# Spreading the keys by heads on Pool in the second attention, and scaling the first batch's probabilities earlier in Pool's queue

## The chip, the cores and the metric

The kernel runs on one core of one Trainium2 chip. The metric is the device time of one execution in microseconds (us). The engines have short names here: PE is TensorE (matmuls), ACT is ScalarE, DVE is VectorE, Pool is GpSimd, SP issues the DMAs. Every engine runs its own queue of instructions in order; they meet only at semaphores.

## What is computed

Four layers, each a cross attention and a feed-forward part, act on x (32 batches of 64 tokens, 128 wide) with a context of the same size. The parts that matter here, cut from the reference:

```python
def _L0_xattn_ref(image_embeds, latents, ...):       # front: 16 heads of 64
    ...
    w = jnp.einsum('bhqd,bhkd->bhqk', q * scale, k * scale)
    w = jax.nn.softmax(w.astype(jnp.float32), axis=-1).astype(q.dtype)
    ...
def _L1_ffn_ref(x, ...):                             # mixture of experts, 2 of 8
    ...
    for _ in range(NUM_ITER):
        ...
        hidden = _gelu(jnp.einsum('tc,tch->th', ctx_e, w1) + b1)
    ...
def _L2_xattn_ref(query, key, value, Wq, bq, Wk, bk, Wv, bv, Wo, bo):
    q = (query @ Wq.T + bq).reshape(B, T, H, D).transpose(0, 2, 1, 3)
    k = (key @ Wk.T + bk).reshape(B, S, H, D).transpose(0, 2, 1, 3)   # H = 16, D = 8
    ...
    scores = jnp.einsum('bhtd,bhsd->bhts', q, k) / np.sqrt(D)
    scores = scores + causal[None, None]
    attn = jax.nn.softmax(scores, axis=-1)
    out = jnp.einsum('bhts,bhsd->bhtd', attn, v)
```

The layers run as x = x + xattn0, x + ffn0, x + xattn1, x + ffn1 (the experts), x + xattn2, x + ffn2, x + xattn3, x + ffn3.

## The kernel before

**Tiling.** A tile is 128 tokens (two batches); there are 16 tiles. Products go to eight PSUM banks. For each bank there is a semaphore that counts fills (`bank_full`) and one that counts emptyings (`bank_free`). The helper `filled` waits until a job's product lies in its bank; `stored` waits until the engine that empties the bank has finished writing the result. Each engine's order is a list written by hand of (kind, lag): in step n, kind works on tile n - lag.

**Front (about 0 to 355 us).** Layer 0 and the attention of layer 1 are one software pipeline with the lists FRONT_PE, FRONT_ACT, FRONT_DVE and FRONT_POOL (L669 to L679). For a tile's two batches b = 0 and 1, PE forms the scores (L812), DVE takes the negated maxima (L1010), ACT the exponentials and their sums (L910), DVE the reciprocals of the sums (L1016, kinds inv0 and inv1), Pool multiplies the exponentials by them (`probs`, L1100, two instructions of 128x512 for each batch, kinds probs0 and probs1), and PE turns the result (L764, kinds turn0 and turn1). A norm is moments on DVE (L507, L512), its root on Pool (two instructions, L517 adds epsilon and L520 takes the power -1/2), and its application on DVE (L526). In a full step Pool's list before is root2, own, ctx (two roots), root1, again, probs0, root0, probs1, bias0, bias1, so five roots stand between the step's own norm and probs0: own, the two of ctx, root1 and again.

**Mixture of experts (about 345 to 620 us).** Chunks of 512 tokens, four chunks and two iterations, with PE, ACT and DVE in hand-written turns. In iteration 0 PE spreads the one-hot routing of a chunk into seven masks (L1556), ACT copies each into SBUF (L1636), DVE multiplies the hidden values by it (L1749). Before the change ACT then waits for its own copy (`stored`) and raises a second semaphore, f1_kept, on which DVE waits.

**Second attention (layer 2, about 600 to 710 us; n == 2 in `attention`).** The last turns of the experts are merged with its first tiles by hand (PE_END, ACT_END, DVE_END, POOL_END, L1285 to L1295); then the steps of ATT_PE, ATT_ACT, ATT_DVE and ATT_POOL (L1299 to L1302) run, and the lists DRAIN_* end it. In a step PE runs s, lnt, v, ot, t, out, av, qk, lnt0: the scores of a tile (L1980 adds the causal mask, L1988 the products), turning the norm (L639), values (L2003), turning the output (L2010), turning the probabilities (kind t, L2018), the output product (L2024), the weighted values (L2037), the projected keys and queries (kind qk, L2046 and L2048, two lags ahead of their use in s), and another norm. ACT runs lnt, v, ot, t, qk, lnt0, s. DVE runs own, max (L2116), tail (L526), add (L576, waits for L2024), s (L2126, scores less their maximum), rsum, stats, av, apply (L526). ACT's kind s is the exponential (L2103), and PE's t waits for it.

Four heads lie in the 32 rows of a PE quadrant, so the keys are stored four times in `km`, each copy multiplied by the column of `head4` that keeps one head's rows. Before the change ACT does this straight from PSUM, four instructions (L2096), and stores the queries with a fifth (L2098):

```python
for h in range(QUAD):
    nc.scalar.activation(km[:, u, :, h, :], ps(k, P, P)..., ACT.Identity,
                         bias=bk2[:, h:h + 1], scale=head4[:, h:h + 1])
nc.scalar.activation(qT2[:, u, :], ps(k, P), ACT.Identity, ...).then_inc(free[k], 1)
```

`bk2` is the key bias times head4, built once on DVE. The fourth attention (n == 3) builds its keys elsewhere (L1933).

## Time and profile before

| | us |
|---|---|
| median of 3 runs (lowest, highest) | 862.83 (862.62, 863.03) |
| the profiled execution's own time | 861.2 |
| its span in the trace | 859.1 |
| PE busy | 809.4 (94% of the span) |
| DVE busy | 625.2 (73%) |
| ACT busy | 581.3 (68%) |
| Pool busy | 271.1 (32%) |

The clock granted to TensorE is 0.998 of full speed over the span. The chain that ended last is PE 60%, DVE 13%, ACT 12%, Pool 8%, issue 5% of the span. Its largest pieces on ACT are the exponentials and the four key copies of the second attention (L2096, 3%), on Pool the roots (L520, 3%) and the scaling of probabilities (L1100, 2%).

To read a row of a timeline: start in us from the span's start, length, engine, line, instruction, output<-inputs, shapes, how many in a row were merged, and in brackets the engine's idle time before it with what ended it. Successive instructions of one engine overlap a little in the records, so the distance of two starts is what one costs its engine.

### The profile page before, as it was taken

The numbers are of one execution on the slowest core, as the hardware profiler recorded it, in microseconds if no ns is written. First come the engines' busy times: TensorE is split into PE (matmuls) and PEld (weight loads), VectorE is DVE, ScalarE is ACT, GpSimd is POOL, SyncE is SP. The second block draws the span as 40 slices with busy tenths as digits, with TensorE's granted clock in tenths as the row PEclk, the third lists the DMA queues.
The fourth block names the chain that finished last, engine by engine and source line by source line (L and its number), as shares of the span: only waits on it lengthen the run. The fifth ranks groups of instructions, "written<-read, shape, count | busy, mean of one in ns | idle before, by whom it ended". The sixth has DMA issues, their size and how long they took to land.

```text
span 859.1 us, 20341 instructions
## 1 busy us (share of the span) xinstructions
PE 809.4 (94%) x7364; PEld 563.9 (66%) x7364; DVE 625.2 (73%) x1588; ACT 581.3 (68%) x1645; POOL 271.1 (32%) x571
## 2 busy tenths in 40 slices
PE   9999999999999999899999999999888889899986
PEld 8887888888888986544444444444555564676652
DVE  5677777777777565676785786685877667799876
ACT  3666676776777766776545585545788879778664
POOL 4355445544444444210000000002034230344455
PEclk9999999999999999999999999999999999999999
DMA  8700000000000000000000000000000000000000
GB/s 339 160 2 2 1 2 2 2 2 1 1 2 2 2 1 2 1 1 0 1 1 0 1 2 0 1 1 0 23 7 3 4 2 1 2 4 3 3 19 34
DMA packets 7887, 13.54 MB, mean 16 GB/s; under 512 B 4342, under 2 KB 5100, under 8 KB 7532
## 3 DMA queue, kind: packets, MB, share of 16 engines
q1 hardware_dynamic: 7788, 12.24, 4.5%
q8 instruction: 60, 0.98, 0.5%
q14 instruction: 39, 0.32, 0.1%
HBM read 11.19 MB, written 1.05 MB: 14 GB/s over the span
## 4 chain that ended last, share of the span: by engine, by line
PE 60%; DVE 13%; ACT 12%; POOL 8%; issue 5%; DMA 0%; DVEq 0%; POOLq 0%; SPq 0%; ACTq 0%
PE psum L1564 10%; PE psum L772 6%; PE psum L812 4%; POOL rstd L520 3%; PE psum L755 3%; PE psum L2018 3%; PE psum L764 3%; ACT arena L2096 3%; POOL arena L1100 2%; PE psum L1573 2%; DVE negmax L1010 2%; PE psum L1550 2%; PE psum L840 2%; ACT arena L910 2%; PE psum L2526 2%
## 5 line engine op out<-in xcount | busy, mean ns | idle before, releaser
L517 POOL TENSOR_TENSOR ve<-mv,epsv 128x1 f32<-128x1 f32 x176 | 36.4, 207 | 508.4 <-DVE mv L512 508.4
L1564 PE MATMUL psum<-arena,w1f 128*128 128x512 f32 x240 | 109.5, 592 | 0.0
L520 POOL TENSOR_TENSOR rstd<-ve,epsv 128x1 f32<-128x1 f32 x176 | 101.7, 578 | 13.8
L910 ACT ACTIVATE arena<-psum,negmax 128x128 f32<-128x128 f32 x256 | 90.5, 408 | 22.2 <-DVE negmax L1010 22.2
L1564 PEld LDWEIGHTS psum<-arena,w1f 128*128 128x128 f32 x240 | 45.5, 190 | 48.7 <-issue 44.3
L1100 POOL TENSOR_TENSOR arena<-arena,rsum 128x512 f32<-128x512 f32 x64 | 65.3, 1040 | 5.6 <-DVE rsum L1016 5.6
L910 ACT ACTIVATION_READ_ACCUMULATOR arena<-psum,negmax 128x1 f32 x256 | 63.4, 248 | 0.0
L1010 DVE TENSOR_REDUCE negmax<-psum 128x8 f32<-128x1024 f32 x32 | 39.2, 1225 | 32.9 <-PE psum L812 32.7
L755 PE MATMUL psum<-arena,sclA 128*128 128x128 f32 x512 | 62.5, 275 | 0.1
L772 PE MATMUL psum<-arena 128*128 128x512 f32 x128 | 61.3, 598 | 0.7 <-DVE arena L1005 0.4
L840 PE MATMUL psum<-prjB,arena 128*128 128x128 f32 x512 | 59.9, 275 | 0.0
L755 PEld LDWEIGHTS psum<-arena,sclA 128*128 128x128 f32 x512 | 59.7, 192 | 0.3 <-ACT arena L964 0.3
L812 PE MATMUL psum<-arena 128*128 128x128 f32 x512 | 59.9, 275 | 0.0
L812 PEld LDWEIGHTS psum<-arena 128*128 128x128 f32 x512 | 58.7, 192 | 1.6 <-issue 1.4
L840 PEld LDWEIGHTS psum<-prjB,arena 128*128 128x128 f32 x512 | 58.5, 192 | 0.2 <-issue 0.2
L576 DVE TENSOR_TENSOR x_tok<-x_tok,psum 128x128 f32<-128x128 f32 x80 | 22.8, 284 | 44.5 <-PE psum L2024 18.6
L526 DVE TENSOR_SCALAR yln<-x_tok,mv,rstd 128x128 f32<-128x128 f32 x128 | 49.1, 395 | 7.6 <-POOL rstd L520 7.3
L649 ACT ACTIVATE lnT<-psum 128x128 f32<-128x128 f32 x96 | 26.5, 281 | 39.2 <-PE psum L639 38.6
L999 DVE COPY arena<-psum 128x512 f32<-128x512 f32 x64 | 42.6, 678 | 7.9 <-PE psum L755 7.8
L2018 PE MATMUL psum<-const,arena 128*128 128x128 f32 x256 | 35.8, 279 | 10.8 <-ACT arena L2103 9.1
L507 DVE BATCH_NORM_STATS2 st<-x_tok 128x6 f32<-128x128 f32 x128 | 36.1, 282 | 13.4 <-DMA x_tok<-in_x_tok 4.8
L2116 DVE TENSOR_REDUCE arena<-psum 128x16 f32<-128x1024 f32 x32 | 39.2, 1225 | 8.6 <-PE psum L1988 8.3
(376 smaller groups left out, 1968.4 us busy)
## 6 DMA issues: line engine op xcount, KB each, us to landing
w<-in_w0qk SPq DMA_DIRECT2D x2, 512.0 KB, 5.0
w<-in_w0vo SPq DMA_DIRECT2D x1, 1024.0 KB, 7.6
cT<-in_cT SPq DMA_DIRECT2D x1, 1024.0 KB, 15.8
out<-x_tok SPq DMA_DIRECT2D x4, 256.0 KB, 2.2
rows<-in_rows SPq DMA_DIRECT2D x1, 836.0 KB, 12.3
x_tok<-in_x_tok SPq DMA_DIRECT2D x1, 768.0 KB, 9.8
ctx_tok<-in_ctx_tok SPq DMA_DIRECT2D x1, 768.0 KB, 10.8
wa<-in_wa SPq DMA_DIRECT2D x1, 768.0 KB, 17.4
```

The lines of the kernel that those rows point to most:

```text
L520: pool.tensor_tensor(rstd[:, u, self.i:self.i + 1], ve[:, u, self.i:self.i + 1], epsv[:, 1:2], ALU.pow) \
L526: nc.vector.tensor_scalar(yln[:, u, self.i, :], src, mv[:, u, self.i, 0:1], rstd[:, u, self.i:self.i + 1], ALU.subtract, ALU.mult).then_in ...
L755: m = nc.tensor.matmul(ps(k, P, j * P), sclA[:, 4 * c + j, :], kvT[:, t.n % 2, :, S:P], start=True, stop=True)
L772: nc.tensor.matmul(ps(a0.bank(job, t)), kvk[:, t.n % 2, b, :], pT0[:, b, 4 * half:4 * half + 4, :], start=True, stop=True).then_inc(full[a ...
L812: m = nc.tensor.matmul(ps(a0.bank(job, t), P, j * P), q0T[:, u, b, h:h + 2, :].rearrange("p h q -> p (h q)"), kvT[:, u, b, :], start=True, ...
L840: m = nc.tensor.matmul(ps(a0.bank("out", t), D), u0T[:, u, h, :], prjB[:, h, :], start=h == 0, stop=h == H0 - 1)
L910: m = nc.scalar.activation(e0[:, b, g, :], ps(k, P, j * P), ACT.Exp, bias=negmax0[:, b, g:g + 1], accum_out=sum0[:, b, g:g + 1])
L999: nc.vector.tensor_copy(q0T[:, t.n % 2, :, 4 * c:4 * c + 4, :], ps(k).rearrange("p (h b q) -> p b h q", h=4, b=2)) \
L1010: nc.vector.tensor_reduce(negmax0[:, b, :], psum[:, 2 * b:2 * b + 2, :].rearrange("p a (g k) -> p (a g) k", g=4), AX.X, ALU.max, negate=Tr ...
L1100: pool.tensor_tensor(p0[:, b, g, :], e0[:, b, g, :], rsum0[:, b, g].unsqueeze(2).to_broadcast((P, 4, P)), ALU.mult).then_inc(a0_probs, 1)
L1564: nc.tensor.matmul(ps(k), w1("e2", j * 384 + arg * D, j * 384 + (arg + 1) * D), f1_Hm[:, n, 2 * j + i, :], start=False, stop=False)
L2018: m = nc.tensor.transpose(ps(k, P, j * P), e2[:, t.n % 2, h:h + 2, :].rearrange("p h k -> p (h k)"), ident)
```

## The change

1. In FRONT_POOL, probs0 moves from behind root1 and again to before them.
2. In the experts' masks ACT no longer waits for its own copy, and f1_kept is gone: DVE waits for the bank's emptying itself (same count, `stored`).
3. In the second attention ACT stores the keys once, with their bias (kT2, 128x128 for each of two tiles in turn). Pool gets a new kind km: it waits for the bank's emptying (which the queries' store raises), from tile 2 on for the scores of the tile before the last, and writes the four copies with one multiplication of 128x512 (kT2 broadcast over heads, head4 broadcast over keys). PE's s also waits for the new semaphore `spread`. km stands second in ATT_POOL, between root and tail; in POOL_END km 0 to 2 stand before root 5, and km 3 after own 5. bk2 and its build go.

```diff
--- before.py
+++ after.py
@@ -675,7 +675,7 @@
         FRONT_DVE = [("add2", 10), ("max0", 4), ("silu", 8), ("max1", 4), ("as", 9), ("own", 0), ("ctx", 1), ("add1", 8), ("again", 6), ("inv0", 4),
                      ("p", 9), ("add0", 5), ("inv1", 4), ("queries", 3), ("apply", 0), ("apply2", 10), ("turn0", 4), ("apply1", 8), ("ctx apply", 1),
                      ("att", 9), ("apply0", 5), ("again apply", 6), ("turn1", 4), ("q3", 3)]
-        FRONT_POOL = [("root2", 10), ("own", 0), ("ctx", 1), ("root1", 8), ("again", 6), ("probs0", 4), ("root0", 5), ("probs1", 4), ("bias0", 6),
+        FRONT_POOL = [("root2", 10), ("own", 0), ("ctx", 1), ("probs0", 4), ("root1", 8), ("again", 6), ("root0", 5), ("probs1", 4), ("bias0", 6),
                       ("bias1", 8)]
         FULL_STEPS = TILES + 4
         LATE = TILES - C1 // P
@@ -1292,14 +1292,15 @@
         DVE_END = [of_last("err"), ("own", 0), ("own", 1), ("apply", 0), ("apply", 1), ("own", 2), ("own", 3), of_last("clamp"), ("apply", 2),
                    ("apply", 3), ("own", 4), of_last("S"), ("apply", 4), of_last("U"), of_last("E"), of_last("P"), ("max", 0), ("s", 0), of_prev("G"),
                    ("max", 1), ("s", 1), ("own", 5), of_prev("Z"), of_last("G"), ("apply", 5), of_last("Z")]
-        POOL_END = [("root", 0), ("root", 1), ("own", 0), ("own", 1), ("root", 2), ("root", 3), ("own", 2), ("own", 3), ("root", 4), ("own", 4), ("root", 5), ("own", 5)]
+        POOL_END = [("root", 0), ("root", 1), ("own", 0), ("own", 1), ("root", 2), ("root", 3), ("own", 2), ("own", 3), ("root", 4), ("own", 4), ("km", 0), ("km", 1),
+                    ("km", 2), ("root", 5), ("own", 5), ("km", 3)]
         END_BANKS = {("ha1A", PREV): 7, ("ha1B", PREV): 5, ("f21", PREV): 4, ("hh1", LAST): 5, ("f110", LAST): 6, ("f111", LAST): 7,
                      ("ha1A", LAST): 5, ("ha1B", LAST): 4, ("f21", LAST): 6, ("xo", PREV): 4, ("xo", LAST): 4}
         ATT_BANKS = {"s0": 0, "s1": 1, "s2": 2, "s3": 3, "lnt": 4, "v": 6, "ot": 7, "t1": 5, "t0": 4, "out": 7, "av": 6, "qk": 7, "lnt0": 5}
         ATT_PE = [("s", 4), ("lnt", 9), ("v", 5), ("ot", 7), ("t", 5), ("out", 7), ("av", 6), ("qk", 2), ("lnt0", 1)]
         ATT_ACT = [("lnt", 9), ("v", 5), ("ot", 7), ("t", 5), ("qk", 2), ("lnt0", 1), ("s", 4)]
         ATT_DVE = [("own", 0), ("max", 4), ("tail", 8), ("add", 7), ("s", 4), ("rsum", 6), ("stats", 7), ("av", 6), ("apply", 0)]
-        ATT_POOL = [("root", 0), ("tail", 7), ("bias", 8), ("own", 1)]
+        ATT_POOL = [("root", 0), ("km", 2), ("tail", 7), ("bias", 8), ("own", 1)]
         ATT_LAST = 9
         DRAIN_PE = [("lnt", 11), ("K", 0), ("av", 14), ("ot", 13), ("v", 15), ("t", 15), ("out", 13), ("lnt", 12), ("ot", 14), ("av", 15), ("out", 14),
                     ("ot", 15), ("out", 15), ("lnt", 13), ("K", 1), ("lnt", 14), ("V", 0), ("lnt", 15)]
@@ -1490,7 +1491,7 @@
         CLOCK_JOBS = {"L": "lg", "H": "h0s", "F": "hh1", "Z": "xo"}
         F1_CLOCK = {('L', 0, 0, None): 4, ('H', 2, 0, 's'): 7, ('H', 3, 0, 's'): 3, ('F', 3, 1, None): 5, ('Z', 3, 1, None): 4}
 
-        f1_masked, f1_kept = sem("f1_masked"), sem("f1_kept")
+        f1_masked = sem("f1_masked")
         spare = [arena[:, 16384:16896], mat(rows, ROWS, "f0_s1"), mat(rows, ROWS, "f0_s2"), ctx_tok[:, 1792:2048],
                  f0w1[:, :], f0w2[:, :, :].rearrange("p c d -> p (c d)"), arena[:, 15360:16128]]
         spare = [x[:, i * C1 // 2:(i + 1) * C1 // 2].bitcast(BF16) for x in spare for i in range(x.shape[1] // (C1 // 2))]
@@ -1499,10 +1500,6 @@
         def masked(c, it, arg):
 
             return len(MASKS) * [at for at, *_ in turns()].index((c, it)) + MASKS.index(arg) + 1
-
-        def held(c, arg):
-
-            return len(MASKS) * c + MASKS.index(arg) + 1
 
         def f1_pe(pe, x):
             kind, c, it, arg = x
@@ -1634,8 +1631,6 @@
                 if c >= 2 and arg == MASKS[0]:
                     act.wait_ge(f1_masked, masked(c - 2, 1, MASKS[-1]))
                 nc.scalar.activation(f1_mask[n][MASKS.index(arg)], ps(k), ACT.Copy).then_inc(free[k], 1)
-                stored(act, f1, f"m{it}{arg}", t)
-                act.sem_inc(f1_kept, 1)
             if kind == "W":
                 for s, job in enumerate(("cwA", "cwB")):
                     k = take(job)
@@ -1745,7 +1740,7 @@
                 i, j = MASKS.index(arg), EC - 1 if arg == "AB" else int(arg[1])
                 stored(dve, f1, f"h{it}{j}", t)
                 if it == 0:
-                    dve.wait_ge(f1_kept, held(c, arg))
+                    stored(dve, f1, f"m{it}{arg}", t)
                 nc.vector.tensor_tensor(f1_Hm[:, n, i, :], f1_H[:, n, j, :], f1_mask[n][i], ALU.mult).then_inc(f1_masked, 1)
             if kind == "err":
                 if it == 0:
@@ -1902,7 +1897,6 @@
         km3 = [x.rearrange("p (i b h k) -> p i b h k", i=TC, b=2, h=QUAD) for x in (
             sclA[:, :, :].rearrange("p h d -> p (h d)"), prjB[:, :, :].rearrange("p h d -> p (h d)"), ctx_tok[:, :], w1f[:, 0:B * S])]
         bk3 = sb("bk3", [P, QUAD])
-        bk2 = sb("bk2", [P, QUAD])
         v3_built = sem("v3_built")
         ahead = {}
         last_tiles = {}
@@ -1961,8 +1955,10 @@
             oT2 = carve(P)
             rs2 = carve(2 * H2).rearrange("p (u h) -> p u h", u=2)
             max2 = carve(2 * H2).rearrange("p (u h) -> p u h", u=2)
+            kT2 = carve(2 * P).rearrange("p (u k) -> p u k", u=2) if late else None
             assert used["n"] <= (24 * C1 if late else ARENA - (2 * 2 * HALF * 18 + HALF + QUAD)), used
             maxed, exped, inverted, spent = (sem(f"a{n}_{x}") for x in ("max", "exp", "rsum", "spent"))
+            spread = sem("a2_spread") if late else None
 
             def on_pe(pe, kind, n_tile):
                 t = At(n_tile)
@@ -1981,6 +1977,8 @@
                     stored(pe, a, "qk", t)
                     if n == 3:
                         kept(pe, "K", t)
+                    else:
+                        pe.wait_ge(spread, t.times(1, 1))
                     keys = km3[t.n // TC][:, t.n % TC, :, :, :] if n == 3 else km[:, u, :, :, :]
                     for i in range(4):
                         r, k = slice(i * 32, (i + 1) * 32), a.bank(f"s{i}", t)
@@ -2090,11 +2088,7 @@
                     if t.n >= 2:
                         filled(act, a, "s3", t - 2)
                     if n == 2:
-                        if t.n == 0:
-                            act.wait_ge(a_half, 4)
-                        for h in range(QUAD):
-                            nc.scalar.activation(km[:, u, :, h, :], ps(k, P, P).rearrange("p (b k) -> p b k", b=2), ACT.Identity,
-                                                 bias=bk2[:, h:h + 1], scale=head4[:, h:h + 1])
+                        nc.scalar.activation(kT2[:, u, :], ps(k, P, P), ACT.Identity, bias=vec("a2_bk"))
                     nc.scalar.activation(qT2[:, u, :], ps(k, P), ACT.Identity, bias=bqs[:, n - 1:n], scale=DH2 ** -0.5).then_inc(free[k], 1)
                 if kind == "lnt0":
                     before.store(act, t)
@@ -2155,6 +2149,15 @@
                 t = At(n_tile)
                 if kind == "root":
                     before.root(pool, t)
+                if kind == "km":
+                    u = t.n % 2
+                    stored(pool, a, "qk", t)
+                    if t.n == 0:
+                        pool.wait_ge(a_half, 2 * (n - 1))
+                    if t.n >= 2:
+                        filled(pool, a, "s3", t - 2)
+                    pool.tensor_tensor(km[:, u, :, :, :], kT2[:, u, :].rearrange("p (b k) -> p b k", b=2).unsqueeze(2).to_broadcast((P, 2, QUAD, S)),
+                                       head4.unsqueeze(1).unsqueeze(3).to_broadcast((P, 2, QUAD, S)), ALU.mult).then_inc(spread, 1)
                 if kind == "tail":
                     tail.root(pool, t)
                 if kind == "bias":
@@ -2175,7 +2178,6 @@
                 nc.vector.tensor_tensor(head4, head8[:, 0:QUAD], head8[:, QUAD:HALF], ALU.add).then_inc(a_half, 1)
                 dve.wait_ge(a_half, 2)
                 nc.vector.tensor_scalar(bk3[:, :], head4, vec("a3_bk"), None, ALU.mult).then_inc(a_half, 1)
-                nc.vector.tensor_scalar(bk2[:, :], head4, vec("a2_bk"), None, ALU.mult).then_inc(a_half, 1)
                 nc.vector.tensor_copy(Vx.rearrange("p u g (r c) -> p (u g) r c", c=9)[:, :, :, DH2],
                                       mat(const, CONST, "half").unsqueeze(1).to_broadcast((P, 4 * HALF, 2))).then_inc(a_built, 2)
```

## Rows read from the trace of the kernel before

**Rows 1.** Busy time by stage; columns: stretch, length, busy us of each engine, PEclk, DMA.

```profile
100.00:345.00 245.00, 241.65 (x1852) 211.61 (x1850) 170.15 (x467) 171.70 (x662) 117.13 (x230) 1.00 0.01 1
...
345.00:600.00 255.00, 248.92 (x964) 119.13 (x964) 183.95 (x358) 157.04 (x283) 18.17 (x38) 1.00 0.00 1
...
615.00:691.00 76.00, 63.10 (x1421) 43.91 (x1421) 54.42 (x131) 62.34 (x166) 24.77 (x65) 1.00 0.03 10
```

**Rows 2.** Waits of the whole run: total us, times, longest.

```profile
PE psum L764 <- POOL arena L1100: 3.5, 12, 1.0
```

**Rows 3.** Timeline of PE, front: start, length, what, idle before it.

```profile
29.71 0.63 PE L764 MATMUL psum<-const,arena 128*128 128x128 f32 x4 [0.98 <-POOL arena L1100]
...
64.73 0.63 PE L764 MATMUL psum<-const,arena 128*128 128x128 f32 x4 [0.37 <-POOL arena L1100]
...
182.55 0.63 PE L764 MATMUL psum<-const,arena 128*128 128x128 f32 x4 [0.16 <-POOL arena L1100]
```

**Rows 4.** Timeline of POOL, one front step.

```profile
176.36 0.19 POOL L517 TENSOR_TENSOR ve<-mv,epsv 128x1 f32<-128x1 f32 x1 [5.25 <-DVE mv L512]
...
180.36 1.04 POOL L1100 TENSOR_TENSOR arena<-arena,rsum 128x512 f32<-128x512 f32 x1
...
183.20 2.04 POOL L1100 TENSOR_TENSOR arena<-arena,rsum 128x512 f32<-128x512 f32 x2
```

**Rows 5.** Timeline of DVE, the same front step.

```profile
178.39 0.19 DVE L1016 RECIPROCAL rsum<-sum 128x8 f32<-128x8 f32 x1
...
183.82 0.50 DVE L526 TENSOR_SCALAR yln<-x_tok,mv,rstd 128x128 f32<-128x128 f32 x1
184.24 1.08 DVE L526 TENSOR_SCALAR yln<-ctx_tok,mv,rstd 128x128 f32<-128x128 f32 x1
```

**Rows 6.** Timeline of ACT, mixture-of-experts stage.

```profile
481.25 2.02 ACT L1636 ACTIVATE rows<-psum 128x512 bf16<-128x512 f32 x3
```

**Rows 7.** Waits between 600 and 715 us.

```profile
PE psum L2018 <- ACT arena L2103: 9.1, 12, 0.8
...
PE psum L2046 <- ACT arena L2098: 1.9, 1, 1.9
...
PE psum L2018 <- ACT lnT L649: 1.6, 1, 1.6
```

**Rows 8.** Timeline of ACT, one step of the second attention.

```profile
651.51 1.51 ACT L2096 ACTIVATE arena<-psum,bk,arena 128x128 f32<-128x128 f32 x4 [0.98 <-PE psum L2048]
...
657.24 1.51 ACT L2096 ACTIVATE arena<-psum,bk,arena 128x128 f32<-128x128 f32 x4 [0.98 <-PE psum L2048]
658.63 0.38 ACT L2098 ACTIVATE arena<-psum,bqs 128x128 f32<-128x128 f32 x1
658.88 0.30 ACT L649 ACTIVATE lnT<-psum 128x128 f32<-128x128 f32 x1
659.04 1.08 ACT L2103 ACTIVATE arena<-arena 128x1024 f32<-128x1024 f32 x1
```

**Rows 9.** Timeline of PE, the same step.

```profile
657.41 0.39 PE L1980 MATMUL psum<-m23b,twiceb 64*128 64x256 bf16 x4
...
660.17 1.09 PE L2018 MATMUL psum<-const,arena 128*128 128x128 f32 x8 [0.79 <-ACT arena L2103]
661.17 0.46 PE L2024 MATMUL psum<-wa,arena 128*128 128x128 f32 x2
```

**Rows 10.** Timeline of DVE, the same step.

```profile
657.99 0.34 DVE L526 TENSOR_SCALAR yln<-x_tok,mv,rstd 128x128 f32<-128x128 f32 x1
...
661.67 0.29 DVE L576 TENSOR_TENSOR x_tok<-x_tok,psum 128x128 f32<-128x128 f32 x1 [1.45 <-PE psum L2024]
```

**Rows 11.** Timeline of POOL, the same step.

```profile
657.97 0.19 POOL L517 TENSOR_TENSOR ve<-mv,epsv 128x1 f32<-128x1 f32 x1 [3.30 <-DVE mv L512]
```

**Rows 12.** Groups of POOL instructions, shapes apart: count, busy us, mean ns, idle before.

```profile
L2634 POOL TENSOR_TENSOR f0w<-f0w 128x256 f32<-128x256 f32 x15 | 10.9, 728 | 0.8 <-DVE f0w L2605 0.5
```

**Rows 13.** Timeline of DVE, end of the mixture-of-experts stage.

```profile
604.87 0.69 DVE L1796 SCALAR_TENSOR_TENSOR prjB<-prjB 128x512 f32<-128x512 f32 x1
```

## The prediction

> **What bounds the kernel now.** I read busy time by stage first, then the waits, then one step of each stage on every engine. The stages differ. In the full front steps and in the experts PE is busy 241.65 of 245 us and 248.92 of 255 us: there only PE's last few waits can be won. In the second attention it is busy 63.10 of 76 us [rows 1]. The clock stands at full speed in all three. Almost all that is idle there is one wait: the turning of probabilities (L2018) waits 12 times for the exponential (L2103), 9.1 us in all, and the first tile's the same way 1.6 us more, put down to the ACT instruction behind it [rows 7]. One step shows why. PE's last product of a step lets ACT begin at 657.24; ACT makes the four key copies, then the queries, then a norm, and only then the exponential at 659.04 [rows 8]. PE, which ran through since 657.41, is out of work 0.79 us before 660.17 [rows 9]. The step lasts 5.735 us (651.51 to 657.24 on ACT [rows 8]); eleven are like it. DVE idles 1.45 us of it and Pool 3.30 [rows 10, 11]. So ACT's four copies lie on the path, and Pool and DVE have room.
>
> **Part 1, the front.** Pool passes five roots in 4.00 us (176.36 to 180.36), then probs0 starts [rows 4]. The sums' reciprocals are there at 178.58 [rows 5], when three of the five roots are done (3 x 0.8 = 2.4, so 178.76). Without root1 and again in front probs0 starts 1.6 us earlier, and PE's wait before L764, 0.16 us in a full step [rows 3], goes. What moves back: root1 and again by 2.04 us. root1 then ends near 181.6; DVE applies it at 183.82 [rows 5]. root0 and probs1 keep their start, since Pool's sum up to them is the same. No DMA is moved. The price of all L764 waits is 3.5 us, 12 times [rows 2]. Two of them are tile 0's, where neither root1 nor again exists: 0.98, and one of 0.37 like that at 64.73 [rows 3]. Of the 2.15 left, 0.37 stands in each of steps 6 (64.73) and 7, and 1.4 in eight later ones. In step 7 DVE's L526 collides with probs1 whatever the order, and the half behind it would wait for DVE anyway; I take nothing there. Gain: 0.37 + 1.3 = 1.7 us; bounds 0 (DVE next in each step) and 2.15.
>
> **Part 2, the masks.** Three mask copies take 2.02 us on ACT, 0.67 each with the wait in it [rows 6]. Were a third of that the wait, 28 masks would free 6 us of ACT; but PE is the bound there and hides it [rows 1]. I take 0; bounds nothing and 0.3 gained (DVE gets each mask a little sooner).
>
> **Part 3, the spread, in a steady step.** ACT loses four copies, 1.39 us (657.24 to 658.63), and gets one like the queries' store, 0.25 (658.63 to 658.88) [rows 8]: the exponential ends 1.14 us earlier, which is more than PE's 0.785. PE then runs through, and the step is 5.735 - 0.785 = 4.95 us. A second ring has about the same length: PE from s to the end of out 3.42 (1.97 for s to ot, 1.45 for t and out [rows 9]), then DVE's add and L2126 and back to s, 1.52; 4.94.
>
> Pool's new instruction is 128x512 with one operand broadcast along its innermost axis, as L1100 is: 1.04 us [rows 4]. The upper bound is two full operands, 0.728 for 128x256 [rows 12], twice that 1.46. From below nothing excludes a shorter one, but nothing points there, and L1100 is nearest; I take 1.04. It starts when the queries' store has ended, near 657.95, which is 0.71 after ACT's start. Behind it wait the root of the tail norm (now at 657.97 [rows 11], then about 659.0) and its two bias additions. That root ends near 659.8, and DVE needs it after its maximum, about 659.9: just in time. PE needs the copies only two steps later, so `spread` costs nothing in a steady step.
>
> But Pool holds DVE up. Beside L1100 from 183.20 on, an application of a norm (L526) that DVE began at 184.24 took 1.08 us where its like take 0.34 to 0.50 [rows 4, 5, 10]. DVE's own L526 of this step begins at 657.99 [rows 10], in the very moment the new instruction starts. I take it that Pool is first: DVE loses about 0.8 us. Its idle time after the shortening is 1.45 - 0.785 = 0.66, so DVE misses by 0.1 to 0.15, and since DVE's lateness is handed on only every second step (the new instruction starts by PE's time, not DVE's), the step is about 5.0. Eleven steps x 0.735 = 8.1 us. At 1.46 half of the 0.42 more goes into the step: 5.21, and 5.8 us.
>
> By the Trainium skill (SBUF — State Buffer, Who interferes with whom) the pair of ports is a lock for a whole instruction and issue order decides who blocks; so if DVE's L526 comes first, Pool waits about 0.3 us and DVE nothing. By that rule the step is 4.95 us, and the gain 8.6. Nothing above hangs on this.
>
> **Part 3, its ends.** At the start the copies are on the path with Pool in it. PE waits 1.9 us for the first queries' store (L2098) [rows 7]; that goes down by 1.1. Then s(0) waits for Pool's 1.04, so it is still about 0.9 early. But DVE is in its chain of additions up to L1796 (604.87 to 605.56 [rows 13]), and km 0 and km 1 may each hold it for 1.04; PE's next product needs that chain and then starts at 607.6, as before. So from nothing to 0.95 here. The exponential of tile 0 loses the 1.14 and its 1.6 us wait [rows 7] nearly goes. Together 1.2 us (lock bites) to 2.1; I take 1.2. At the end one L2018 wait is 0.45 (the twelfth: 9.1 less 11 x 0.785) and goes. Km 3 stands behind own 5, near 618.5; s(3) comes after 622: no cost. The dropped build of bk2 is one small DVE instruction, hidden by PE: nothing.
>
> **Sum.** 1.7 + 0 + 8.1 + 1.2 + 0.45 = 11.4 us. The profiled execution took 861.2 (span 859.1), so 849.8; the median of the runs is 1.63 above it, 862.83, so **851.4 us**.
>
> **Rivals.**
> - *The lock doesn't bite* (DVE first each time, start won in full): 8.6 + 0.45 + 2.1 + 1.7 = 12.9, with the front's and masks' upper bounds 13.6: **849.5**. For it: DVE's L526 and Pool's start differ by under 0.1 us. Against: L526 beside L1100 was the one that stretched, in this order of starts. Chance 0.16.
> - *DVE becomes the bound.* The new instruction is dearer (1.46), or DVE is held twice a step: step 5.2, nothing at the start, nothing in the front: 5.8 + 0.45 = 6.3: **856.5**. For it: DVE has only 0.66 us to give. Chance 0.16.
> - *Not what it says*: PE's wait only changes its name, since the tail's root, behind km, holds DVE and with it the next exponential. Then the front alone is left: **861.2**. Against: 0.1 us of slack counts as none, but the ring would have to grow by 0.7. Chance 0.03.
> - *Slower.* The new instruction reads keys broadcast in the middle axis. If Pool took it as four pieces of 1.04, 4.16 us, Pool's step would be 1.6 of roots, 0.9 of biases and 4.16, 6.6 us, and DVE's L526 held for it: 11 x (6.6 - 5.74) = +9.5, less 3 elsewhere: **869**. It decides from about 3.1 us for the instruction (half of its excess goes into the step, and 3.3 us are won elsewhere). Against: L1100's broadcast cost nothing visible. Chance 0.04.
>
> **How the numbers follow.** The forecast (step 4.95 to 5.05) has 0.61. The range reaches from a microsecond below the first rival, 848.5, to the second, 856.5; outside it lie no effect, slower, and what is beyond either end. About 0.2% (1.7 us) is what a measurement here can tell from no change: faster 0.93, same 0.03, slower 0.04.
>
> **What would show it.** In the new profile: L764 no longer waits for Pool after tile 1; in the second attention the starts of ACT's key store are 5.0 us apart; the L2018 waits for L2103 are gone and the wait of DVE for L2024 falls from 1.45 to near 0; the new Pool instruction takes 1.04; DVE's L526 beside it takes 1.1. PE's busy time in all stages is unchanged. Wrong would be: steps above 5.2 us, PE waiting for Pool in s beyond the first two tiles, Pool's roots on the chain of the second attention, or new PE waits in the experts near 603 to 610 us.

## The result and the profile after

The changed kernel took 848.21 us (median of 4 runs, 846.98 to 849.67), the kernel before beside it 862.73: ratio 0.983 [0.9815, 0.9849]. In a second set it was 847.97 (5 runs) against 862.47, ratio 0.983 [0.981, 0.985]. Both gains are 14.5 us. The prediction was 851.4, a gain of 11.4, and its range ended at 848.5.

The page of the profiled execution (its own time 849.67), first lines, clock row and chain:

```profile
span 847.5 us, 20310 instructions
...
PE 808.6 (95%) x7364; PEld 566.2 (67%) x7364; DVE 634.7 (75%) x1587; ACT 563.1 (66%) x1597; POOL 286.8 (34%) x587
...
PE 70%; DVE 13%; ACT 8%; issue 4%; POOL 4%; DMA 1%; DVEq 0%; POOLq 0%; SPq 0%; ACTq 0%
```

PE's work is the same (809.4 before). ACT gave up 18 us and Pool took 16. In the chain, PE rose from 60% to 70% and ACT fell from 12% to 8%. Of these only ACT's fall goes with the second attention: the page of the front's order alone (below) has PE at 71% and ACT still at 12%.

**The front.** PE's timeline, the step that answers to the last row of [rows 3]:

```profile
173.42 1.06 PE L829 MATMUL psum<-f0w,arena 128*128 128x128 f32 x8
180.67 1.04 PE L764 MATMUL psum<-const,arena 128*128 128x128 f32 x8
184.17 1.04 PE L764 MATMUL psum<-const,arena 128*128 128x128 f32 x8
193.46 1.06 PE L829 MATMUL psum<-f0w,arena 128*128 128x128 f32 x8
```

The eight turns of L764 are now one piece, with no wait in the middle. From L829 to L829 the step takes 20.04 us (193.46 - 173.42). Before, by the same rows, it took 20.36:

```profile
174.53 1.06 PE L829 MATMUL psum<-f0w,arena 128*128 128x128 f32 x8
...
181.79 0.60 PE L764 MATMUL psum<-const,arena 128*128 128x128 f32 x4
...
194.89 1.06 PE L829 MATMUL psum<-f0w,arena 128*128 128x128 f32 x8
```

So a wait that the record gives as 0.16 us [rows 3] was worth 0.32. The two halves show why. Eight products in one piece take 1.04 and four take 0.60, so one start follows the next after (1.04 - 0.60) / 4 = 0.11, and the second half could start 0.44 after the first. Before, it started 0.76 after it (182.55 - 181.79), 0.32 late. The first half's record of 0.60 reaches 0.16 past the moment at which the next product could have started, and the idle time in brackets is counted from the end of that record.

**The second attention.** All engines in one step, the rows that matter, in order of time:

```profile
638.27 0.37 ACT L2091 ACTIVATE arena<-psum,vecs 128x128 f32<-128x128 f32 x1 [0.97 <-PE psum L2046]
638.53 0.36 ACT L2092 ACTIVATE arena<-psum,bqs 128x128 f32<-128x128 f32 x1
638.66 0.39 PE L1976 MATMUL psum<-m23b,twiceb 64*128 64x256 bf16 x4 [0.32 <-DVE arena L2120]
...
638.94 1.06 ACT L2097 ACTIVATE arena<-arena 128x1024 f32<-128x1024 f32 x1
...
638.97 1.04 POOL L2159 TENSOR_TENSOR arena<-arena 128x512 f32<-128x512 f32 x1 [1.29 <-ACT arena L2092]
...
639.24 0.86 DVE L526 TENSOR_SCALAR yln<-x_tok,mv,rstd 128x128 f32<-128x128 f32 x1
...
640.40 1.04 PE L2016 MATMUL psum<-const,arena 128*128 128x128 f32 x8
...
640.51 1.23 DVE L2110 TENSOR_REDUCE arena<-psum 128x16 f32<-128x1024 f32 x1
...
641.17 0.45 POOL L620 TENSOR_TENSOR x_tok<-x_tok,crow 128x128 f32<-128x128 f32 x1
...
641.65 0.34 DVE L526 TENSOR_SCALAR yln<-x_tok,mv,rstd 128x128 f32<-128x128 f32 x1
...
641.90 0.28 DVE L576 TENSOR_TENSOR x_tok<-x_tok,psum 128x128 f32<-128x128 f32 x1
642.10 1.22 DVE L2120 TENSOR_TENSOR arena<-psum,arena 128x1024 f32<-128x1024 f32 x1
...
643.18 0.37 ACT L2091 ACTIVATE arena<-psum,vecs 128x128 f32<-128x128 f32 x1 [0.97 <-PE psum L2046]
```

ACT starts the exponential 0.67 us into its step (638.27 to 638.94), where it took 1.80 before (657.24 to 659.04 [rows 8]). PE's L2016 (L2018 before) waits for nothing. DVE's L576, which waited 1.45 us [rows 10], follows at once. Pool's new instruction takes 1.04 us, and DVE's L526 beside it 0.86 instead of 0.34. PE shows a new wait, for DVE's subtraction (L2120), at 619.64, then in every second step, from 648.29 to 662.76 in each, and ahead of the last two. Here are its waits between 600 and 700 us:

```profile
PE psum L1976 <- DVE arena L2120: 3.0, 9, 0.8
...
PE psum L2044 <- ACT arena L2092: 0.7, 1, 0.7
```

The 9.1 and 1.6 us before L2018 are gone, and of 1.9 before the first queries' store 0.7 is left [rows 7]. The steps, as the distance of one L1980 (now L1976) to the next, from tile 3 on:

```
before: 5.36 5.59 5.74 5.73 5.74 5.73 5.74 5.73 5.74 5.75 5.97 5.34   sum 68.16 us (623.52 to 691.68)
after:  4.44 4.94 4.72 4.92 4.72 4.91 4.84 4.80 4.83 4.70 4.69 4.70   sum 57.21 us (619.64 to 676.85)
```

A steady step fell from 5.735 to 4.82 on average (the seven from 629.02 to 662.76), not to 5.0. The last three take 4.70; from the first of them on DVE has one norm less to do.

**The clock.** The first profiled execution of the changed kernel lost some microseconds late in the run, and a second one didn't. Here are the same stretches of both (columns: stretch, length, busy us of PE, its loads, DVE, ACT, Pool, then granted clock, DMA share, GB/s); first, then second:

```profile
718.00:721.00 3.00, 1.92 (x15) 1.56 (x14) 1.76 (x6) 1.11 (x1) 0.92 (x3) 1.00 0.01 3
721.00:724.00 3.00, 2.54 (x12) 2.29 (x11) 1.15 (x5) 1.25 (x3) 1.67 (x4) 0.61 0.00 0
...
814.00:817.00 3.00, 3.00 (x12) 2.48 (x11) 2.70 (x22) 1.45 (x3) 0.86 (x2) 0.50 0.01 3
```

```profile
718.00:721.00 3.00, 1.82 (x13) 1.33 (x11) 2.01 (x7) 0.90 (x2) 1.21 (x3) 1.00 0.01 3
721.00:724.00 3.00, 2.57 (x32) 1.72 (x32) 2.05 (x8) 1.47 (x4) 1.66 (x5) 1.00 0.00 0
...
814.00:817.00 3.00, 3.00 (x28) 1.14 (x30) 2.35 (x12) 2.07 (x8) 0.72 (x1) 1.00 0.01 3
```

At 721 us and again at 814 TensorE ran at the lower of its two levels, 1.2 instead of 2.4 GHz, for 3 to 4 us; the row before the first fall shows PE busy 1.92 of 3 us. The second execution has nearly the same row (1.82 of 3) and no fall. Its span is 844.2 us, 14.9 less than the 859.1 of the kernel before, whose profiled execution has no such stretch either. (In the last few microseconds, when PE has no products left, the clock is low in every one of these traces; that delays no product and isn't counted here.) These two can be set beside each other point by point:

```
point (start of the instruction)                 before    after     difference in all
first scaled-probability turn, L764              29.71     29.85     +0.14
front, L829 near the end of its full steps       335.48    333.25    -2.23
L829 after the first expert chunk's masks        363.14    360.43    -2.71
first projected keys of the second attention     601.81    599.09    -2.72
scores of tile 3 (L1980 / L1976)                 623.52    619.66    -3.86
scores 12 steps on                               691.68    676.85    -14.83
last output product in the drain (L2024 / L2022) 703.44    688.92    -14.52
end of span                                      859.1     844.2     -14.9
```

The front gave 2.37 us (from its own first turn), the masks 0.48, the start of the attention 1.14, the twelve steps 10.97, and the rest next to nothing.

### The profile page after: what moved, and what is told of

Read it like the earlier page. It is cut to its first block, busy times and chain, and to the rows that moved or that the text cites. A ratio compares the mean times of both kernels' runs of the same rounds, so it can differ in the third digit from the quotient of the medians.

```text
span 847.5 us, 20310 instructions
## 1 busy us (share of the span) xinstructions
PE 808.6 (95%) x7364; PEld 566.2 (67%) x7364; DVE 634.7 (75%) x1587; ACT 563.1 (66%) x1597; POOL 286.8 (34%) x587
## 3 DMA queue, kind: packets, MB, share of 16 engines
HBM read 11.19 MB, written 1.05 MB: 14 GB/s over the span
## 4 chain that ended last, share of the span: by engine, by line
PE 70%; DVE 13%; ACT 8%; issue 4%; POOL 4%; DMA 1%; DVEq 0%; POOLq 0%; SPq 0%; ACTq 0%
PE psum L1561 10%; PE psum L772 6%; PE psum L812 6%; PE psum L840 6%; PE psum L755 5%; PE psum L764 3%; PE psum L1547 3%; ACT arena L910 2%; PE psum L2016 2%; PE psum L1570 2%; PE psum L1986 2%; PE psum L2528 2%; PE psum L2405 2%; DVE arena L2120 2%; PE psum L1588 2%
## 5 line engine op out<-in xcount | busy, mean ns | idle before, releaser
L517 POOL TENSOR_TENSOR ve<-mv,epsv 128x1 f32<-128x1 f32 x176 | 35.7, 203 | 422.7 <-DVE mv L512 422.7
L526 DVE TENSOR_SCALAR yln<-x_tok,mv,rstd 128x128 f32<-128x128 f32 x128 | 56.6, 454 | 7.9 <-POOL rstd L520 7.5
L576 DVE TENSOR_TENSOR x_tok<-x_tok,psum 128x128 f32<-128x128 f32 x80 | 22.6, 283 | 25.4 <-PE psum L900 13.6
L2120 DVE TENSOR_TENSOR arena<-psum,arena 128x1024 f32<-128x1024 f32 x32 | 39.0, 1217 | 0.2
```

The costliest lines, as they stand in the source:

```text
L526: nc.vector.tensor_scalar(yln[:, u, self.i, :], src, mv[:, u, self.i, 0:1], rstd[:, u, self.i:self.i + 1], ALU.subtract, ALU.mult).then_in ...
L2120: nc.vector.tensor_tensor(e2[:, u, :, :].rearrange("p (a h) k -> p a h k", h=QUAD), psum[:, 0:4, 0:QUAD * S].rearrange("p a (h k) -> p a h ...
```

## The experiments

**Only the front's order** (the kernel before with this one edit):

```diff
-FRONT_POOL = [..., ("ctx", 1), ("root1", 8), ("again", 6), ("probs0", 4), ("root0", 5), ...
+FRONT_POOL = [..., ("ctx", 1), ("probs0", 4), ("root1", 8), ("again", 6), ("root0", 5), ...
```

> The kernel before with only the reordered Pool list of the front. Theory: the profile of the changed kernel reaches line L829 every 20.04 us in the full steps where it was 20.36, so a wait that the records show as 0.16 us was worth 0.32 (the record of the matmul before it runs 0.16 past the moment at which the next one could start). Eight such steps give 2.1 us; in all 2.1 to 2.3 us faster than before. Rival (my prediction): the wait is worth what is shown, 1.7 us. A third: the gain is only there together with the other parts, then under 1 us.

Measured: 860.05 us (12 runs) against 863.04 (23 runs), ratio 0.9956 [0.994, 0.9973], a gain of 3.0 us between 2.3 and 5.2. In its trace the front takes 303.39 us from the first L764 (29.51) to the L829 near its end (332.90). Before, it was 305.77 (29.71 to 335.48), and in the changed kernel 303.40. So the front's edit is worth 2.38 us, and the other parts neither help nor hurt it. Six full steps from 134 to 256 us take 20.04 instead of 20.36, but the next one takes 20.44 instead of 20.18, in this kernel and in the changed one: 0.26 us are given back there.

**Only the masks** (the kernel before; DVE waits for ACT's store of the mask itself, and ACT's own wait and `f1_kept` go):

```diff
-                stored(act, f1, f"m{it}{arg}", t)
-                act.sem_inc(f1_kept, 1)
...
-                    dve.wait_ge(f1_kept, held(c, arg))
+                    stored(dve, f1, f"m{it}{arg}", t)
```

> The kernel before with only the masks' part (ACT does not wait for its own copy, DVE waits for the bank). Theory: 0.5 us faster, all of it between 350 and 365 us, where DVE and ACT are behind for a moment, and PE hides the rest; the mask copies on ACT stand 0.53 us apart rather than 0.67. Rival (my prediction): nothing, 0 to 0.3.

Measured: 863.05 against 863.04, ratio 0.9994 [0.998, 1.001]. The times can't show half a microsecond. Its trace has three stretches of lowered clock (near 346, 730 and 830 us), so it can't show it either.

**The front's order put back** in the changed kernel, which leaves the masks and the spread:

```diff
-FRONT_POOL = [..., ("ctx", 1), ("probs0", 4), ("root1", 8), ("again", 6), ("root0", 5), ...
+FRONT_POOL = [..., ("ctx", 1), ("root1", 8), ("again", 6), ("probs0", 4), ("root0", 5), ...
```

> The changed kernel with the front's Pool list put back as it was (spread and masks stay). Theory: the parts add up, so 12.0 to 12.6 us faster than before, and the second attention's step still 4.8 us. Rival: the parts feed on each other, and it is under 11 us.

Measured: 850.95 us (6 runs), ratio 0.9854 [0.983, 0.988], so 12.1 us of the gain are left. Its trace settles the masks. From the L829 at 335.62 to the one at 362.81 it takes 27.19 us, the changed kernel 27.19 (333.24 to 360.43), while the kernel before took 27.66 and the kernel with the front's order alone 27.65. The masks give 0.47 us, all of it in the first chunk. PE there, in the kernel before and then here:

```profile
352.13 1.13 PE L829 MATMUL psum<-f0w,arena 128*128 128x128 f32 x8 [0.17 <-ACT rows L1636]
353.48 1.13 PE L790 MATMUL psum<-lnT,f0w 128*128 128x128 f32 x8 [0.23 <-ACTq L653]
```

```profile
352.25 1.13 PE L829 MATMUL psum<-f0w,arena 128*128 128x128 f32 x8 [0.32 <-DVE arena L1028]
353.21 1.06 PE L790 MATMUL psum<-lnT,f0w 128*128 128x128 f32 x8
```

The wait before L829 isn't where the gain lies: L829 comes 6.73 us after the one ahead of it before, and 6.72 here, held by DVE's L1028 in place of ACT's mask copy. The gain is the wait before L790, which needs a norm that ACT stores between its mask copies: from L829 to L790 it is 1.35 us before and 0.96 here, 0.39 less, and the rest follows within L790.

The spread alone wasn't tried; it is what is left beside the front's order and the masks.

**Three of the four key copies left out from tile 2 on** (the kernel before; nothing on Pool, so the keys of three heads of each quad stay as they were):

```diff
-                        for h in range(QUAD):
+                        for h in range(QUAD if t.n < 2 else 1):
                             nc.scalar.activation(km[:, u, :, h, :], ...
```

> The kernel before, but from tile 2 on ACT writes only the first of the four key copies of the second attention (the other three keep the data of tiles 0 and 1, so this leaves out three quarters of the keys' spread); nothing goes to Pool. Theory: ACT's exponential is 3 x 0.3475 = 1.04 us earlier, more than PE lacks, and without the lock the steady step is PE's own, 4.70 to 4.79 us as in the kernel with km behind the root. So the shorter step is ACT's relief alone. Rival (my prediction's size): 4.95 us, the old step less the wait that the records show.

Measured: 850.91 us (one run; the kernel before beside it 862.31), and steps of 4.69 to 4.70 us (one is 4.93). PE shows no wait in such a step, and nothing was done to DVE or Pool. DVE still waits for PE:

```profile
642.42 0.33 PE L2010 MATMUL psum<-const,arena 128*128 128x128 f32 x1
642.59 1.06 PE L2018 MATMUL psum<-const,arena 128*128 128x128 f32 x8
```

```profile
644.06 0.29 DVE L576 TENSOR_TENSOR x_tok<-x_tok,psum 128x128 f32<-128x128 f32 x1 [0.41 <-PE psum L2024]
```

So without ACT's copies the step is 4.70 us, 1.035 under the 5.735 of before, and not the 0.785 that the wait's bracket gave. Of the difference, 0.94 is at this wait: here L2018 starts 0.17 us after L2010, before it started 1.11 after (659.06 to 660.17). Another 0.07 is at the instruction ahead, which started 0.45 after the values (658.61 to 659.06) and here 0.38 (642.04 to 642.42); it had no bracket at all. It needs bank 7, which the queries' store empties (both jobs have that bank in ATT_BANKS), and that store ended at 659.01, late behind the same copies. The last 0.02 is between L2018 and L2024.

What sets the 4.70? Not PE alone. PE's mask product (L1980, L1976 in the changed kernel) may start only when DVE has read the last scores out of the same banks (L2126, L2120). In the second attention it starts 1.27 to 1.28 us after DVE's instruction does in every full step of the kernel before, of the changed kernel and of this one, and 0.37 to 0.40 after the product ahead where no bracket is shown. In the fourth attention, where DVE's instruction lies further back, 0.23 to 0.26 is enough:

```profile
741.79 0.33 PE L639 MATMUL psum<-const,yln 128*128 128x128 f32 x1 [0.24 <-ACT lnT L649]
742.05 0.39 PE L1976 MATMUL psum<-m23b,twiceb 64*128 64x256 bf16 x4
```

So 0.11 us or a little more of waiting for DVE hides in each step of 4.70, and PE's own step would be about 4.6, an estimate. The 4.70 is the ring of PE and DVE: 2.72 us from L1980 to L2024 (640.84 to 643.56), 0.50 to L576, 0.20 to L2126, 1.28 to the next L1980.

**Pool's new instruction behind the first root** (the changed kernel):

```diff
-ATT_POOL = [("root", 0), ("km", 2), ("tail", 7), ("bias", 8), ("own", 1)]
+ATT_POOL = [("root", 0), ("tail", 7), ("km", 2), ("bias", 8), ("own", 1)]
```

> The changed kernel with km one place later in Pool's steady list, behind the root of the tail norm. Theory (the lock of Pool's 1.04 us instruction on DVE sets every second step): DVE's L526 behind the statistics then takes 0.34 and not 0.86 to 1.05, DVE has slack again, PE's waits of 0.20 to 0.32 for L2120 go, and every step is 4.72 us, where it was 4.72 and 4.91 in turn: 1.0 us faster than the changed kernel (0.5 to 2). Rival: the ring of PE and DVE is as long without the lock, and the time is the changed kernel's within 0.3 us. If the later km came too late for PE it would be slower.

> km behind the root of the tail norm, again. Theory: 1.0 to 1.3 us faster than the changed kernel on the same chip (between 610 and 677 us 1.2 us were seen). Rival: the same, if the stretches of half clock decide.

Measured: 847.13 us (6 runs), ratio 0.9818 [0.979, 0.984], and in the second set 847.20, ratio 0.9819 [0.980, 0.984]. That can't be told from the changed kernel by the times. In the trace it can: all steady steps but one are 4.69 to 4.70 us (one is 4.81, in the second trace 5.10), and the twelve together with the one ahead of them take 59.89 us, where the changed kernel takes 61.12. Pool, then DVE, in one step:

```profile
658.84 0.19 POOL L517 TENSOR_TENSOR ve<-mv,epsv 128x1 f32<-128x1 f32 x1 [1.27 <-DVE mv L512]
...
659.62 1.04 POOL L2159 TENSOR_TENSOR arena<-arena 128x512 f32<-128x512 f32 x1
```

```profile
658.87 0.34 DVE L526 TENSOR_SCALAR yln<-x_tok,mv,rstd 128x128 f32<-128x128 f32 x1
...
659.62 1.23 DVE L2110 TENSOR_REDUCE arena<-psum 128x16 f32<-128x1024 f32 x1
660.76 0.40 DVE L526 TENSOR_SCALAR yln<-x_tok,mv,rstd 128x128 f32<-128x128 f32 x1
661.50 0.29 DVE L576 TENSOR_TENSOR x_tok<-x_tok,psum 128x128 f32<-128x128 f32 x1 [0.34 <-PE psum L2022]
```

The new instruction now lies beside DVE's maximum out of PSUM, which takes 1.23 us with it and 1.22 without. Neither L526 is held for long (0.34, and 0.40 beside the first bias addition), and DVE has 0.34 us (by the bracket) to spare again. The Trainium skill (SBUF — State Buffer, Who interferes with whom) says that a reduction never takes the shared ports on this chip while the scalar form can; the traces agree: 1.23 for the reduction, 0.86 for L526.

**The new instruction last in Pool's step:**

```diff
+ATT_POOL = [("root", 0), ("tail", 7), ("bias", 8), ("own", 1), ("km", 2)]
```

> The changed kernel with km last in Pool's steady list, behind both biases. Theory: the lock now falls on DVE's other L526 (the one between the maximum and L576), or on nothing if Pool is through by then. In the first case it takes about 1 us there, right before L576 and L2120, with no idle time between: mean step 4.85 to 5.0 us, longer than the changed kernel's 4.82. In the second it is 4.70 as with km behind the root. Rival (the order in Pool's list matters for its own roots alone): 4.70.

Measured: 847.33 us (one run), steps of 4.69 to 4.70 without exception. Pool, then DVE:

```profile
639.96 1.04 POOL L2159 TENSOR_TENSOR arena<-arena 128x512 f32<-128x512 f32 x1
```

```profile
640.27 0.82 DVE L526 TENSOR_SCALAR yln<-x_tok,mv,rstd 128x128 f32<-128x128 f32 x1
641.01 0.29 DVE L576 TENSOR_TENSOR x_tok<-x_tok,psum 128x128 f32<-128x128 f32 x1
```

Here an L526 is still held, by 0.42 to 0.48 us in every step (0.82 instead of 0.34 or 0.40), and it costs nothing, because DVE has about that much to spare: from start to start its instructions of a step add up to 4.20 us without a hold, 0.50 under 4.70, and this hold, measured in the same way, takes 0.49 (640.27 to 641.01, less 0.25). So it isn't the hold as such that costs the changed kernel its 0.12 us a step, but how long it is: there it is more than the 0.50, as shown below. Of the theory's two cases neither came: the L526 is held and the step is 4.70 all the same.

**The new instruction done twice**, the second writing the same values once the first is done:

```diff
                    pool.tensor_tensor(km[:, u, :, :, :], ..., ALU.mult).then_inc(spread, 1)
+                    pool.wait_ge(spread, 2 * t.n + 1)
+                    pool.tensor_tensor(km[:, u, :, :, :], ..., ALU.mult).then_inc(spread, 1)
...
-                        pe.wait_ge(spread, t.times(1, 1))
+                        pe.wait_ge(spread, t.times(2, 2))
```

> The changed kernel with Pool's multiplication done twice per tile, one after the other. Theory (DVE's L526 is held until Pool is through, and that is on the ring in every second step): L526 takes near 2.1 us, two steps last 9.63 + 1.1, so the mean is 5.3 to 5.4 us instead of 4.82; if DVE gets in between the two, L526 stays at 1.05 and the second is felt by the root behind it, 4.9 to 5.1. Rival (no part for the lock): 4.82 as before.

Measured: 853.06 us (one run), every steady step 5.15, which lies between the numbers of the two theories. That is 0.33 more than the changed kernel's 4.82, for 1.12 us more on Pool (from 640.79 to 641.91 for one). DVE's rows:

```profile
641.06 0.86 DVE L526 TENSOR_SCALAR yln<-x_tok,mv,rstd 128x128 f32<-128x128 f32 x1
...
643.84 0.40 DVE L526 TENSOR_SCALAR yln<-x_tok,mv,rstd 128x128 f32<-128x128 f32 x1 [0.29 <-POOL rstd L520]
```

and PE's:

```profile
644.49 0.49 PE L2044 MATMUL psum<-cT,wa 128*128 128x128 f32 x2 [0.17 <-DVE x_tok L576]
```

The hold is as long as before (0.86; the second instruction doesn't meet an L526). What binds is another ring, inside one step: ACT's stores, Pool's two instructions, the tail's root, DVE's L526 and L576, PE's next L2044, ACT's stores again. The second instruction's 1.12 us lie in it whole, so with one this ring is about 5.15 - 1.12 = 4.03 us, an estimate, 0.67 below 4.70. In the changed kernel it has room.

**One microsecond more on ACT**, a copy of 128x1024 ahead of the exponential (the changed kernel):

```diff
                     nc.scalar.activation(qT2[:, u, :], ps(k, P), ...).then_inc(free[k], 1)
+                    if n == 2 and t.n:
+                        nc.scalar.activation(spill, cT[:, 0:8 * P], ACT.Copy)
```

> The changed kernel with one more ACT instruction of about 0.95 us (128x1024 into a spare tile, nothing reads it) behind the queries' store, ahead of the exponential. Theory: ACT is then about as late as before the change (1.39 + 0.25 before, 0.25 + 0.25 + 0.95 now), so PE waits for L2097 again and the step is 5.735 - 0.2 = 5.5 to 5.6 us, although Pool still spreads the keys. Rival: something else that the change brought makes the step short, and it stays under 5.1.

Measured: 857.39 us (one run), steps of 5.55. PE waits for the exponential again:

```profile
644.67 0.33 PE L2009 MATMUL psum<-const,arena 128*128 128x128 f32 x1
645.66 1.09 PE L2017 MATMUL psum<-const,arena 128*128 128x128 f32 x8 [0.66 <-ACT arena L2100]
```

This is the calibration of a bracket. The step is 0.85 us over 4.70, the record says 0.66, and the starts, 0.99 us apart where 0.17 would do, say 0.82. The copy costs ACT 0.95 (637.89 to 638.84), so ACT's ring without it is 5.55 - 0.95 = 4.60 us, only 0.10 below 4.70. ACT isn't far from binding again.

**The changed kernel again, and a try to hold the clock.** The second set ran the changed kernel, the kernel with the new instruction behind the root, and that one with three extra clock-keeping products at two places (its edit of ATT_POOL, as above, is left out here):

```diff
             if kind == "f2 turn":
+                if n_tile == 0:
+                    fill(pe, f2, "lnt", t)
+                    keep_clock(pe, f2.bank("lnt", t), 2)
                 tail_f2.turn(pe, t)
...
+                    if n == 3 and t.n == 0:
+                        keep_clock(pe, k, 1)
                     lnT_of(pe, before, t)
                     nc.tensor.matmul(ps(k, P), wgt(n, "q")...
```

> The changed kernel once more, on the same chip as the two below. Theory: 14.5 us faster than before, with runs spread over 3 us, since in some of them TensorE is granted half its clock for 3 to 4 us once or twice, at places that change from run to run (near 345, 603, 720 and 815 us so far), 1.4 us each.

> km behind the root, and three more idle-time matmuls of the kernel's own kind (keep_clock) near 720 us, where PE idled 0.64 and 0.46 us before the clock fell in the changed kernel's profile: two ahead of the first norm to be turned, one ahead of the first queries of the last attention. Theory: the low stretch at 720 does not come, and the median is 0.3 to 1.4 us below that of km behind the root. Rival: the low stretches come by chance at other places as well and the median is the same within 0.5 us.

Measured: 847.97 us for the changed kernel, 847.20 for the first variant, 846.47 for the one with the extra products (5 runs each), ratios 0.9831 [0.981, 0.985], 0.9819 [0.980, 0.984] and 0.9813 [0.979, 0.983]. The three intervals overlap. In the last one's trace the clock stays up at 720 and 813 us, but it falls once near 344. The stretches per profiled run are:

```
run                         span us   lowered stretches, near
before                      859.1     none
after                       847.5     721, 815
after, second time          844.2     none
front's order alone         857.8     605
masks alone                 863.0     346, 730, 830
front's order put back      848.9     816
behind the root             844.9     344
behind the root, again      845.2     814
last in the step            845.2     814
one copy                    849.1     724, 816
done twice                  850.9     818
one us more on ACT          855.2     344
with extra products         845.1     344
```

Each costs some 1.5 to 1.7 us. At 764.93 us in the changed kernel's second trace and 764.03 in the variant's (the start of L2528 in both) the variant is 0.90 ahead, and at DVE's last instruction (840.94 and 841.75) it is 0.81 behind; there the one stretch cost 1.7. The two traces of the changed kernel are 3.26 apart at that instruction, for two stretches, and the two of the variant 1.46 at 602 us, for the one near 344. So single spans can't be compared to better than that, and whether the extra products help stays open. The variant with the new instruction behind the root is about 0.9 us better up to that point, by its trace; by times alone it is not shown to be.

## Why the prediction fell short

**The mechanism was in the main as said.** ACT's copies were on the path, the exponential now comes 1.13 us earlier into ACT's step (1.80 to 0.67) against 1.14, the L2018 waits are gone, DVE's wait for PE fell from 1.45 to nothing, Pool's instruction takes 1.04, the start of the attention gave 1.14 against 1.2, and PE's busy time is unchanged. "Not what it says" and "Slower" didn't come, nor did the 5.2 us of "DVE becomes the bound", though its name fits: from 629 to 663 us the changed kernel's DVE has no wait at all. Nor did "The lock doesn't bite": the hold is there (0.86 to 1.05 us against 0.34), and DVE's late subtraction does reach PE.

**The step that failed is "the step is 5.735 - 0.785 = 4.95 us".** It took what the record calls idle for what the wait costs. Leaving out copies with nothing else changed gave 4.70, and so did both moves of Pool's instruction. The wait was worth 1.035 a step (0.94 at the wait, 0.07 in front of it, 0.02 behind), and "PE, which ran through since 657.41" passed over that 0.07. Over eleven steps that is 2.75 us more than was said; the hold takes some of it back, below. The second ring, given as 4.94, is there, but it was summed from rows' lengths in the same way: from start to start it is 4.70, and it is what bounds the step once ACT is out of the way.

**What the hold costs was under-sized.** The prediction put the step 0.05 over the step without a hold, as half of a miss of 0.1 to 0.15, because DVE's lateness would be handed on only every second step. It is 0.12 on average, so 0.07 a step or 0.8 us in eleven more than was said. DVE's rows of the changed kernel show how it comes about. DVE runs its instructions of a step without a gap, and from start to start they take 4.20 us plus what the held L526 takes beyond its 0.25: 0.53 in one step (L526 from 639.24, the next instruction at 640.02) and 0.72 in the next (643.96 and 644.93). That gives 4.73 and 4.92, and PE's steps there are 4.72 and 4.91. Later the hold is 0.62 to 0.65 and the steps are 4.80 to 4.84. DVE can give 0.50 and has to give 0.62 on average, and the difference is the 0.12. The prediction gave DVE too much room (0.66) and too long a hold (0.8), and then halved the miss, which in the traces goes into the steps whole.

The length of the hold follows from where Pool starts, 0.07 to 0.27 us ahead of L526, and Pool starts by ACT's stores, which follow PE. So what DVE hands on comes back to it one step later. The list of waits that ended last in the changed kernel leads from Pool's instruction over its bias additions (L620, ended 641.62) to DVE's second L526 at 641.65. That isn't a wait: this L526 starts 1.14 us after the maximum (640.51 to 641.65), and behind the root it does the same (659.62 to 660.76) although the bias additions run until 661.49 there. So the bias additions have no part in the 0.12.

**The front** was said to be worth 1.7 with an upper bound of 2.15, and gave 2.37. The bound was the sum of the brackets, and a bracket was no upper bound: 0.16 was worth 0.32 in each full step from 134 to 256 us. The term failed in the same way as the step.

**The masks** were put at 0 with 0.3 as the bound; they gave 0.47, in the first chunk. The prediction took "PE is the bound there and hides it" from one window of 255 us, PE busy 248.92 [rows 1]. The gain lies in one of PE's waits, which that window averages away.

Together: 0.67 from the front, 0.47 from the masks, 2.4 from the steps and the drain (10.97 against 8.1 + 0.45), and -0.06 from the start make 3.5 us, and 11.4 + 3.5 = 14.9, the difference of the two spans without a lowered clock. The medians differ by 14.5, since runs of either kernel meet such stretches. The range was too narrow at its lower end chiefly for one reason: the front and the steps, its two largest terms, were read with the same gauge, so they were off together, and it treated them as if each could only be off by itself. It was missed by 0.3 us, less than the masks alone gave.

## What to carry to other kernels

Price a wait on PE by the distance of two starts, against the distance of the same two where nothing waits (in another tile, or another stage), and not by the idle time in the bracket; when every term is read in one way, widen the range for that way of reading. When an engine with room takes over work, look for what its new instruction stands in front of in its own queue, and beside what it runs on the neighbour: here the place behind one root, beside a reduction out of PSUM, made the long hold disappear, as the trace shows. Count what the engine beside it can give, from start to start: a hold shorter than that is free, as with the instruction last. Small gains of a microsecond are read at fixed points of two traces; the whole time hides them behind stretches of lowered clock.

## What was unexpected of the hardware

PE's recorded idle time was shorter than what the wait cost in each case with both numbers: 0.16 for 0.32, 0.79 for 0.94, 0.66 for 0.82, each time by about 0.16 us, after a turning product of 128x128. That is what the record of one such product (0.33) is longer than the distance to the next where nothing waits (0.17). After another kind the bracket was right: L1976 is given 0.32 at 638.66, and starts 0.59 us after the product ahead (638.07), where 0.23 to 0.26 is enough in the fourth attention, so 0.33 or a little more. And a wait can have no bracket at all: the 0.11 of the same instruction in steps of 4.70, and the 0.07 of L2010.

TensorE fell to its lower level at 721 us in one execution of a program and stayed up in the next, with PE busy 1.92 and 1.82 of the 3 us before. Eleven of the thirteen profiled executions have one to three such stretches of 3 to 4 us, between 342 and 834 us.

The held L526 ends with Pool's instruction wherever it began: 0.09 us after it in the changed kernel (639.24 + 0.86 against 638.97 + 1.04), 0.09 after it with the instruction last (640.27 + 0.82 against 639.96 + 1.04). Pool had started first each time, by 0.27 and 0.31 us. By the Trainium skill (SBUF — State Buffer, Who interferes with whom) the engine that issues first keeps the shared ports for its whole instruction; the traces agree, with these two numbers. Its reverse is in the first trace of the changed kernel: DVE's L1744, with both inputs in SBUF, started 0.17 us ahead of Pool's L517, which took 0.56 where 0.19 is usual and ended 0.06 after it:

```profile
352.90 0.67 DVE L1744 TENSOR_TENSOR arena<-arena,rows 128x512 f32<-128x512 f32 x1
```

```profile
353.07 0.56 POOL L517 TENSOR_TENSOR ve<-mv,epsv 128x1 f32<-128x1 f32 x1 [4.63 <-DVE mv L512]
```

The copies that ACT lost cost 0.35 us each and the store that took their place 0.25, of the same 128x128 out of PSUM: from start to start 657.24 to 658.63 for four [rows 8], and 638.27 to 638.53 for L2091. The four read both a scale and a bias by partition, the one only a bias.
